# A first decoder layer turned to feature-major tensors in three stages: z and y by features, split output products, norms spread through memory

## The reference, cut to what matters

```python
x = hidden_states * rsqrt(mean(hidden_states ** 2, -1) + eps) * norm_w
x, z = split(x @ in_proj_w.T + in_proj_b)              # 1536 each
x = silu(causal_depthwise_conv4(x) + conv_b)
xp = (x @ x_proj_w.T + x_proj_b).reshape(B, L, 24, 1 + 2 * 64)
dt, Bs, Cs = xp[..., 0], xp[..., 1:65], xp[..., 65:]
Bs, Cs = Bs / norm(Bs), Cs / norm(Cs)
...
h = alpha[..., None, None] * h + (1.0 - alpha)[..., None, None] * u_t   # step over 256 tokens
y = einsum('bhs,bhsd->bhd', C_t, h)
...
out = (Y * silu(z)) @ out_proj_w.T + out_proj_b
x1 = layernorm(hidden + (hidden + res_gate * out))
```

## Time and profile before

| what | us |
|---|---|
| median of 3 runs | 5150.24 |
| lowest and highest run | 5149.49, 5150.84 |
| profiled execution | 5107.47 |
| its span, first to last instruction | 5105.8 |
| PE busy | 4036.0 (79%) |
| DVE busy | 2823.3 (55%) |
| ACT busy | 1618.9 (32%) |
| POOL busy | 1412.4 (28%) |
| mean granted clock of PE | 0.891 |

### The profile page before, as it was taken

One profiled execution on the slowest core, in us unless ns is written; L12 is line 12 of the kernel. 1 busy time (PEld: TensorE's weight loads), 2 busy tenths in 40 slices (PEclk: granted clock), 3 DMA queues, 4 the chain that ended last, 5 costly groups with the idle time before them and its releaser, 6 DMA issues. The chain is left out here.

```text
span 5105.8 us, 61033 instructions
## 1 busy us (share of the span) xinstructions
PE 4036.0 (79%) x19166; PEld 3090.8 (61%) x19166; DVE 2823.3 (55%) x5022; ACT 1618.9 (32%) x3311; POOL 1412.4 (28%) x1213
## 2 busy tenths in 40 slices
PE   7985999979999796852995886677778778837993
PEld 6874777767777544642442775455556556715772
DVE  6664344443444344972223674899999855532335
ACT  4342222232222110020221565555555422203431
POOL 0001200000000003755102440899999800011002
PEclk9997999989999898965997898898889989968996
DMA  4224622232122343133996534332222021133324
GB/s 129 104 100 175 198 81 79 65 103 83 58 86 74 109 187 129 45 142 103 339 318 223 167 121 150 117 138 93 82 79 78 28 99 52 49 97 112 116 95 120
DMA packets 434226, 603.28 MB, mean 118 GB/s; under 512 B 115142, under 2 KB 310791, under 8 KB 424849
## 3 DMA queue, kind: packets, MB, share of 16 engines
q1 hardware_dynamic: 388240, 490.99, 29.3%
q0 software_dynamic: 43232, 101.96, 6.0%
q10 hardware_dynamic: 2592, 8.39, 0.4%
HBM read 436.56 MB, written 206.54 MB: 126 GB/s over the span
## 5 line engine op out<-in xcount | busy, mean ns | idle before, releaser
L2216 PE MATMUL d_py<-d_h,d_ident 128*128 128x256 f32 x2048 | 543.5, 425 | 176.4 <-POOL d_h L2056 156.7
L2064 POOL TENSOR_TENSOR d_dBu<-d_B,d_dtu 128x1024 f32<-128x1024 f32 x256 | 596.8, 2362 | 115.4 <-DMA d_dtu<-dtu 115.4
L2216 PEld LDWEIGHTS d_py<-d_h,d_ident 128*128 128x128 f32 x2048 | 431.1, 214 | 288.3 <-POOL d_h L2056 184.6
L715 PE MATMUL a_pB<-a_uhi,a_whi 128*128 128x512 f32 x1152 | 487.7, 423 | 40.9 <-DVE a_ulo L598 40.8
L715 PE MATMUL a_pB<-a_uhi,a_wlo 128*128 128x512 f32 x1152 | 461.6, 401 | 0.0
L715 PE MATMUL a_pB<-a_ulo,a_whi 128*128 128x512 f32 x1152 | 458.7, 398 | 0.0
L2102 ACT ACTIVATE d_ph<-d_dt,d_A 128x255 f32<-128x255 f32 x1024 | 425.7, 460 | 0.1
L2162 DVE TENSOR_TENSOR_SCAN d_ph<-d_ph,d_dBu 128x1024 f32<-128x1024 f32 x160 | 365.7, 2286 | 18.4 <-POOL d_dBu L2064 12.0
L1004 POOL TENSOR_TENSOR b_kv<-b_c 128x128 f32 (+11 forms) x256 | 100.3, 431 | 864.6 <-DMA b_c<-ctx_turned 860.7
L715 PEld LDWEIGHTS a_pB<-a_uhi,a_whi 128*128 128x128 f32 x1152 | 223.4, 194 | 83.3 <-issue 31.7
L682 DVE SCALAR_TENSOR_TENSOR a_W<-a_pG,a_cB,a_M 128x256 f32<-128x256 f32 (+1 forms) x384 | 142.7, 413 | 229.7 <-PE a_pG L736 129.9
(11 more groups left out here) (459 smaller groups left out, 9409.5 us busy)
## 6 DMA issues: line engine op xcount, KB each, us to landing
c_gu<-w_gu SPq DMA_DIRECT2D x64, 768.0 KB, 5.1
a_wraw<-w_bc SPq DMA_DIRECT2D x24, 1536.0 KB, 5.9
a_alall<-alpha SPq DMA_DIRECT2D x24, 1024.0 KB, 5.9
slots<-a_zeros POOLq DMA_DIRECT2D x64, 256.0 KB, 3.4
c_wd<-w_down SPq DMA_DIRECT2D x64, 256.0 KB, 6.1
c_xb<-slots SPq DMA_DIRECT2D x64, 256.0 KB, 8.0
slots_y<-c_y POOLq DMA_DIRECT2D x64, 256.0 KB, 7.1
f_w1r<-w SPq DMA_DIRECT2D x64, 256.0 KB, 2.6
```

The costliest lines, as they stand in the source:

```text
L715: ins = nc.tensor.matmul(out, a[:, k, cols], b[:, k, ts], start=(k == 0 and n == 0), stop=(k == F - 1 and n == 2))
L2064: pool.tensor_tensor(dBu[c % RB][:, :, :], B_sb[i][:, q * G:(q + 1) * G, :], dtu_sb[i][:, f, :].unsqueeze(1).to_broadcast([P, G, L]), ALU. ...
L2216: ins = nc.tensor.matmul(py[f % 2][:, 0:L], ident_sb[:, :], h_sb[c % RH][:, n, :], start=False, stop=(q == Q - 1 and n == G - 1))
```

## The change

It does the following.

- Project: z is made by features, as px is: for each block f 12 matmuls with 256 columns right behind px(f), and ACT makes silu with the bias of its partition straight from PSUM. DVE's addition goes. The bias is loaded as 12 columns and not spread over the partitions. PE waits before pz(f) until f-1 silus are made. z is stored by features. The order of the weight groups changes.
- Scan, units: for each batch one block of output for both heads at steps 1, 3, 5, 7. The u of a head is the weights (64 columns of them) and W the moving side with 128 columns; y comes out by features, head h on partitions 64h to 64h+63. W has four buffers. DVE evicts a batch at steps 3, 5, 7 and after 7, with one multiplication of 256 columns by rC_all, the reciprocal norms spread over the partitions. SP makes that in the way of alpha: store as rows, wait, two loads of 64 partitions; it does so first in a unit, ahead of u by tokens and the weights. y is stored by features.
- Scan, weights: B and C halves come as two loads of 768 KB into a buffer of half the size, C behind B's split, and in a unit behind the alphas.
- Scan, starts: u comes in 24 chunks of one block with six buffers; PE, ACT and DVE don't wait for the constants at the stage's start, which SP sends after 18 chunks are split. In the second half's first step PE makes the 24 B projections between the steps of unit 11 and the sums of their squares later; the zero stores wait for each other and take their zeros from another tile, in 512-byte pieces.
- Out: y and z are loaded by features, multiplied in two pieces and split in high and low parts (ACT, DVE), the weights as well, piece by piece in four buffers. PE makes 72 float32r matmuls a batch and no transposes of y. The products of batches 0 and 1 stand ahead of norm(0) on ACT and DVE, and those of b+2 go behind norm(b). The loads of batch b+3 leave when b+1 is split.

```diff
+                    pe.wait_ge(s_z, b * F + max(f - 1, 0))
+                    if first and f % 4 == 0:
+                        ready(pe, 3 + f // 4)
+                    for k in range(KD):
+                        ins = parts(pz[f % 2][:, 0:L], (w_hi, w_lo), slice(DI + f * P, DI + (f + 1) * P), (xnT_hi, xnT_lo), slice(0, L), k)
+                    ins.then_inc(s_pz, 1)
...
+                        act.wait_ge(s_pz, b * F + g + 1)
+                        nc.scalar.activation(z_sb[:, g, :], pz[g % 2][:, 0:L], ACT.Silu, bias=bz_sb[:, g:g + 1]).then_inc(s_z, 1)
...
-    KC = 2
+    KC = 1
...
+    UBUF = 6
...
+            def norms(cur):
+                sp.wait_ge(s_rC, cur + 1)
+                alone(sp, tick_sp)
+                sp.dma_start(norm_rows.rearrange("r t -> t r"), rC[:, :, :].rearrange("p h c -> p (h c)"), allow_slow_non_contiguous=True).then_inc(s_rC_stored, 16)
+                sp.wait_ge(s_rC_stored, cur * 16 + 16)
+                alone(sp, tick_sp)
+                for h in range(2):
+                    sp.dma_start(rC_all[h * S:(h + 1) * S, :], norm_rows[h * TT:(h + 1) * TT, :].rearrange("c t -> (c t)").partition_broadcast(S)).then_inc(s_rC_all, 16)
...
             def step(half, cur, nxt, parity=None, first=False):
...
+                if cur is not None:
+                    norms(cur)
...
-                        weights(0 if last else pair + 1, nxt + 1, 1 - into)
+                        b_weights(0 if last else pair + 1, 1 - into)
                     if not first:
                         spread(nxt, into)
+                    if parity is not None or nxt < UNITS - 1:
+                        c_weights(0 if last else pair + 1, nxt + 1)
...
+                            pool.dma_start(rows[bass.ds(r * P, P), :].rearrange("p (c n) -> p c n", n=P), zeros).then_inc(s_clear, 16)
+                            pool.wait_ge(s_clear, (r + 1 + stores) * 16)
...
-                    if i >= 2 and i % 2 == 0:
-                        b = i // 2 - 1
+                    if i >= 3 and i % 2 == 1 or i == NI:
+                        b = (i - 3) // 2 if i < NI else NBH - 1
                         if b == 0:
                             dve.wait_ge(s_out, cur * 16)
+                            dve.wait_ge(s_rC_all, cur * 32 + 32)
+                        dve.wait_ge(s_y, cur * NBH + b + 1)
+                        nc.vector.tensor_tensor(y_sb[:, b * L:(b + 1) * L], py[:, 0:L], rC_all[:, b * L:(b + 1) * L], ALU.mult).then_inc(s_ye, 1)
...
+                def output(b):
+                    pe.wait_ge(s_W, cur * NI + 2 * b + 2)
+                    pe.wait_ge(s_ye, cur * NBH + b)
+                    for lo, w0, w1, c, start, stop in ((0, 0, P, 0, True, True), (P, P, 2 * P, 0, True, False), (P, 2 * P, 3 * P, 1, False, True)):
+                        for h in range(2):
+                            r = slice(h * S, (h + 1) * S)
+                            ins = nc.tensor.matmul(py[r, lo:lo + P], ut_sb[at][:, 2 * b + c, r], W[(2 * b + h) % 4][:, w0:w1], start=start, stop=stop)
+                    ins.then_inc(s_y, 1)
...
+                if first:
+                    for j in range(BLK * F):
+                        slots[j // (BLK * F // NI) + 1].append(j)
...
+                        for n, (v, w) in enumerate(((y_hi[i], w_hi), (y_hi[i], w_lo), (y_lo[i], w_hi))):
+                            ins = nc.tensor.matmul(po[c][:, :], v[:, k, at], w[:, k, :], start=(k == 0 and n == 0), stop=(k == F - 1 and n == 2))
```

More of the change, by code:

```diff
@@ L477, in step @@
                                  .rearrange("(c p) n -> p c n", p=P)).then_inc(s_ut, 16)
+                    if first and half == 0:
+                        consts()
                     sp.wait_ge(s_wl, nxt * 2 + 2)
@@ L764, in project @@
                         ins.then_inc(s_pB, 1)
-                    if k == 3 and n >= 1:
-                        if n == 1 and cur is not None:
+                    late = first and cur is not None and n <= 2
+                    if k == 3 and n >= 1 and not (late and n == 1):
+                        if n == (2 if late else 1) and cur is not None:
                             pe.wait_ge(s_rootC, nxt)
+                        if n == 1 and cur is None:
+                            pe.wait_ge(s_first, 32)
                         if n == BLK + 1:
                             pe.wait_ge(s_arg, nxt + 1)
+                        if late:
+                            norms(nxt, 0)
                         norms(nxt, n - 1)
@@ L791, in step @@
                             scores(i // 2 + 1)
[L792 removed]
+                        if i % 2 == 1:
+                            output(i // 2)
                 if first:
[L794 removed]
+                    for j in range(BLK * F, NQ * F):
                         project(j)
@@ L834, in pipelined, with ahead @@
                     products(2 * r + 1 + i, r + i, (1 + i) % 2)
-                    norm(2 * r + i, i)
+                    norm(2 * r + i, i, r)
             products(NB - 1, NB // 2 - 1, 1)
             for i in range(2):
-                norm(NB - 2 + i, i)
+                norm(NB - 2 + i, i, NB // 2 - 1)
+        def ahead(eng, products, norm):
+            for i in range(2):
+                products(i, 0, i)
+            with eng.Fori(0, NB // 2 - 1) as r:
+                for i in range(2):
+                    norm(2 * r + i, i, r, lambda r=r, i=i: products(2 * r + 2 + i, r + 1, i))
+            for i in range(2):
+                norm(NB - 2 + i, i, NB // 2 - 1, None)
         def rows(a, b, n):
@@ L889, in norm @@
                     nc.scalar.copy(oT[:, c, :, :].rearrange("p k t -> p (k t)"), px[c][:, :]).then_inc(s_oT, 1)
-            pipelined(act, products, norm)
+            ahead(act, products, norm)
         @block.vector
```

280 lines of the change are left out of this document (140 added, 140 removed).

## The result

The median of four runs went from 5149.86 to 5062.52 us (5057.23 to 5075.15), a ratio of 0.9832 with an interval of 0.9814 to 0.9849: 87 us less. The forecast was 100 less, 5050, and the range of 5005 to 5100 holds the result. The span of the profiled execution is 5055.6 us against 5105.8, only 50 less, so the 5007 forecast for it was missed by 50. A second profile of the kernel before (first experiment) shows why.

| stage, us | before | before again | after | after again |
|---|---|---|---|---|
| ssm0_project | 439.1 | 440.3 | 444.8 | 444.3 |
| ssm0_scan | 1286.5 | 1286.5 | 1245.1 | 1240.6 |
| ssm0_out | 241.6 | 241.4 | 191.9 | 194.4 |
| norm_route (same code) | 203.1 | 239.7 | 228.3 | 235.4 |
| mix_project (same code) | 431.1 | 435.9 | 442.0 | 436.2 |

What follows compares the result with a forecast made beforehand. TensorE's instruction stream was taken to bound the long scan runs and last stage, chains of waits the stretches between. +7 - 30 - 8 - 16 - 11 + 8 - 50 = -100: 5007 us profiled, 5050 median; range 5005 to 5100.

Steps and rivals of the forecast that it cites:

- Project: Project stage: feature-wise z adds a wait for silu and smaller matmuls, less a smaller bias load; +7 us (0 to +12).
- Output blocks and W's wait: Steady scan units: four split-shape output blocks replace eight, -30 us (-64 to +18); four W buffers remove a wait, -8.
- halves in turn: Rival, scan output blocks: the two heads' array halves run one after another, block 1.54 us, total 5098; chance 14%.
- drains: Rival, scan units: each of sixteen shape switches costs a matmul's whole tail, 0.16 us; 28 us in all, 5078; chance 8%.
- loads that do not overlap: Rival, output blocks: loading one half's weights does not overlap the other's pass; block 2.8 us, +144, total 5224; chance 3%.
- First half's start: Scan, first half: smaller u chunks with six buffers let TensorE go on near 494 instead of 510; -16 us (-8 to -22).
- the gate terms hold the starts: Rival, both scan starts: gate terms, not the splits of u, hold them, so the change fails there; 5070; chance 3%.
- Second half's start: Scan, second half: splits without waits and fewer products left shorten the stretch from 82 to 69; -11 us (-5 to -18).
- Last unit: Scan's last unit: no products hide the norms' store and load, VectorE waits at the first eviction; +8 us.
- Out stage: Out stage: split matmuls, no y transposes, seven rounds in 125 us (-46), prologue -4; -50 us (-38 to -58).
- Norm chain: Scan units: norms' detour through memory is hidden, 3 to 5 us to spare; rival that it is late: 5105, chance 6%.
- Zero stores: Scan, first half: 80 zero stores, one at a time, take some 330 us beside the units and cost nothing.

Runs made afterwards that it cites:

- first experiment: Two controls: the kernel before, unchanged, profiled a second time, 5148.67 us; the kernel after, unchanged, 5057.22 us, ratio 0.9832.
- experiment 4: Kernel after with output products in the old form (W as weights, u moving): 5076.87 us, 0.9860; also with two products ahead of the last norm group: 5038.4, 0.9798.
- experiment 5: Kernel after with two buffers for W instead of four, and the wait this needs: 5081.54 us, ratio 0.9868.
- experiment 8: Kernel after with ScalarE's first two evictions ahead of the gate terms at the start of both halves: 5034.13 us, ratio 0.9799.
- Experiment 9: Kernel after with two products before the last norm group, early evictions at the starts, and a PSUM bank per output in the last unit: 4992.24 us, 0.9694.
- experiment 6: Kernel after with the reciprocal norms stored twice, one store behind the other, before they are loaded: 5253.1 us, ratio 1.0200.

## Why the prediction was right, and where it was off

- **Project**, forecast +7: +5.7 and +4.0 in the two pairs. The wait for z was 1.97 a batch, worked out as 2.2, and took the place of 12.0 us of waits for dt.
- **Output blocks and W's wait**, forecast -30 and -8. A unit without half clock went from 48.5 to 46.5, 2.0 less, 43 us in 22 units: a little more than the 38. Of the 2.0 the wait for W is 0.37 and the output blocks with their changes of shape 1.6, where the sum had 1.3. It had both sides a little low. The block alone came to 1.00 and not 0.94. And of the eight old blocks, all taken at 0.67, four stand behind scores and took 0.69 and 0.09 to leave. (The sum also adds the 0.09 of scores apart to the forecast's block and not to those of its two bounds; with it the halves in turn would lose 1.1 a unit and not 0.8.) The rivals with halves in turn (1.5 a block), with drains and with loads that do not overlap fall by the block alone; experiment 4 shows the form's price without the clock. What failed is that I held the number of units at half clock constant: it rose from 9 to 17 or 18, 1.6 each, and gave 13 to 14 us back. So the units brought 22 x 1.30 = 29 for the forecast's 38. That the whole came out within 13 us of the forecast is in part luck: the blocks' better price covers 5 us of this loss. That W's buffers were worth only the 0.46 seen was right for the difference, but as a condition they are worth 1.56 a unit (experiment 5).
- **First half's start**, forecast -16: -9.4 and -12.0. Two terms were mis-sized. The 24 splits took 26.4 us (467.7 to 494.1) and not 20 to 24, 1.1 us a chunk and not 0.69: ScalarE waited 10.8 us for chunks ten times in spite of six buffers. And the constants were there at 491.5 on the old scale and not at 484, since they are sent after a count of splits. The 7.3 of gate terms stayed (498.6 to 506.0). The rival that the gate terms hold the starts was half right: both held in turn, and experiment 8 takes out another 11.2.
- **Second half's start**, forecast -11: -10.3, interval 71.75.
- **Last unit**, forecast +8: +7.0. Experiment 9 turns it into -1.3.
- **Out stage**, forecast -50: -49.7 and -47.0. Pitch 17.9 (18.0), first part 51.5 instead of 55 (-4 forecast), the clock as assumed, and 262 GB/s in a round with loads for the 250 assumed.
- **Norm chain** with 3 to 5 us to spare: 2.5 in experiment 6, and one wait of 3.2 in the steady units of after. **Zero stores** at nothing: right one at a time and with the stop in each unit, though they took 529 us (488 to 1017) and not 330, all of the first half's units; 38 us when together, and 0.6 to 0.9 a unit of the first half once TensorE has no stop.
- Sum of the terms: 5.7 - 28.6 - 9.4 - 10.3 + 7.0 - 49.7 = -85.3 for -100. The 15 that are missing are the units (9) and the first start (7), the others nearly cancel. The comparison with the profiled execution alone would have given -50; the untouched stages account for the difference.

## What to carry to other kernels

A short stop of TensorE in a busy stretch costs its own length and may cost as much again in clock (1.36 and 1.6 us here). So look first for a product that can be put in front of the wait: two products moved by a few lines gave some 50 us, as much as the out stage, the largest part of the change. When a stage is made tighter, count what its remaining stops do to the clock, and take a second profile before a difference in a stage is believed.

A detour through memory in a queue with a few us to spare is paid for by whatever else is in flight: pace bulk stores by an event of that chain.

## What the runs showed of the hardware

Half clock behind a stop of TensorE depends on more than the stop. Units of the second half, of eleven, with a stretch at 1.2 GHz of 3.4 us (granted clock 0.97 to 1.00 in their window), and the length of a unit without one:

| kernel | stops in a unit, us | unit without, us | units with it |
|---|---|---|---|
| before | 1.36, and 0.4 for W | 48.5 | 4 |
| after | 1.36 | 46.5 | 9 |
| after, evictions ahead of the gate terms | 1.36 | 46.5 | 8 |
| after, two buffers for W | 1.36, and 1.56 for the eviction | 48.1 | 3 |
| after, old form of output | 1.36 | 47.8 | 1 |
| after, one product ahead | 0.67 | 45.8 | 0 |
| after, two products ahead | 0 | 45.2 | 0 |
| after, two products ahead, old form of output | 0 | 46.5 | 0 |

With the same stop, after has it in nine units and the old form of output in one. This does not show that the form is the cause: with two buffers for W the form is the new one (64 columns of weights in each output matmul), and there are three. The lengths of the units differ too, and with them the moment at which each stop comes. The eleven units are not independent trials either. In after the stretch begins 1.6, 1.2, 0.9 and 0.6 us after TensorE goes on, in four units one behind the other; the fifth has none, and then it begins at 1.6 again. With the old form the first unit of each half has the stretch, and the ten behind it, alike to 0.1 us in the second half, have none. So the moment of the stop is a rival to the form that no run here tells apart; a run with the old form and another length of unit would. What the runs do show is that without a stop, or with one of 0.67 us, no unit of the second half had it.
